# Causal mask of a two-layer decoder's self-attention: mask matmuls replaced by constant rows (first pass) and by a GpSimd select (second pass), constant rows copied on chip, the values' projection spread over the loop

## The reference

```python
# layer 0: 16 heads of 16, ALiBi bias; layer 1: 16 query heads, 4 key/value heads, no bias
x = x + attn0(layernorm(x))        # softmax(q k / 4 + slope*(j - i) + causal) v, then @ wo + bo
x = x + xattn0(layernorm(x), ctx)
x = x + moe0(layernorm(x))
x = x + attn1(layernorm(x))        # softmax(where(j > i, -inf, q k / 4)) v
x = x + xattn1(layernorm(x), ctx)
x = x + moe1(layernorm(x))
```

## Time and profile before

| | |
|---|---|
| runs | 1432.47, 1433.92, 1435.11 us; median 1433.92 |
| profiled execution | 1430.22 us, its span 1428.4 us, mean TensorE clock 0.906 |
| busy | PE 84%, PEld 59%, DVE 63%, ACT 47%, POOL 32% of the span |
| layer 0 self-attention | span 0 to about 240 us |
| layer 1 self-attention | span about 606 to 820 us |

### The profile page before, as it was taken

One profiled execution on the slowest core, in us unless ns is written; L12 is line 12 of the kernel. 1 busy time (PEld: TensorE's weight loads), 2 busy tenths in 40 slices (PEclk: granted clock), 3 DMA queues, 4 the chain that ended last, 5 costly groups with the idle time before them and its releaser, 6 DMA issues.

```text
span 1428.4 us, 25941 instructions
## 1 busy us (share of the span) xinstructions
PE 1205.4 (84%) x8255; PEld 839.2 (59%) x8255; DVE 897.5 (63%) x2622; ACT 673.9 (47%) x1412; POOL 461.7 (32%) x708
## 2 busy tenths in 40 slices
PE   3789998986699999848898768778787778999988
PEld 2467766765366666535565545555555554688855
DVE  3646654665333222266876578999999884566557
ACT  2245534321211111114454479999999991333310
POOL 1010101245611111111222234456555554255510
PEclk8899999997799999968999968987887888999999
DMA  6585751411211111144442030000000003354454
GB/s 139 115 208 120 148 150 39 148 38 60 87 45 45 45 52 46 48 139 123 116 140 71 3 122 2 2 32 32 24 21 20 32 32 122 95 158 158 158 177 144
DMA packets 71889, 123.43 MB, mean 86 GB/s; under 512 B 12630, under 2 KB 54998, under 8 KB 68255
## 3 DMA queue, kind: packets, MB, share of 16 engines
q1 hardware_dynamic: 59756, 91.76, 24.5%
q0 software_dynamic: 10272, 28.39, 5.5%
q10 hardware_dynamic: 1728, 1.61, 0.3%
HBM read 77.14 MB, written 44.19 MB: 85 GB/s over the span
## 4 chain that ended last, share of the span: by engine, by line
PE 53%; issue 12%; ACT 10%; DVE 9%; DMA 7%; POOL 6%; SPq 3%; POOLq 0%; DVEq 0%; ACTq 0%
PE ps L227 16%; PE ps L1092 15%; PE ps L1109 7%; ACT work L1806 5%; DMA W<-q_parts 3%; ACT work L1811 2%; POOL xs_scratch L1423 2%; DMA k_parts<-work 2%; PE ps L1101 2%; PE ps L1077 2%; DVE work L580 2%; POOL work L1837 2%; PE ps L444 2%; PE ps L1657 1%; SPq L791 1%
## 5 line engine op out<-in xcount | busy, mean ns | idle before, releaser
L1092 PE MATMUL ps<-W,work 128*128 x628 | 227.9, 496 | 1.4 <-issue 1.2
L1806 ACT ACTIVATE work<-ps,work 128x512 f32<-128x512 f32 x256 | 211.4, 873 | 8.8 <-POOL work L1837 7.2
L1441 POOL DMA_INDIRECT ys_scratch<-work x118 | 113.2, 960 | 260.7 <-DVE work L1285 112.4
L1742 DVE TENSOR_REDUCE work<-ps 128x1 f32<-128x512 f32 x256 | 172.9, 679 | 29.1 <-PE ps L1651 28.4
L580 DVE TENSOR_REDUCE work<-ps 128x2 f32<-128x512 f32 (+1 forms) x192 | 128.7, 684 | 91.3 <-PE ps L447 91.0
L1335 DVE TENSOR_TENSOR work<-work,ps 128x128 f32<-128x128 f32 (+1 forms) x118 | 49.7, 421 | 199.5 <-ACT work L1404 198.9
L688 ACT ACTIVATE work<-ps 128x512 f32<-128x512 f32 x192 | 114.6, 602 | 101.0 <-PE ps L467 98.6
L271 POOL TENSOR_TENSOR rstd<-ve,half 128x1 f32<-128x1 f32 x96 | 56.0, 587 | 294.8 <-DVE ve L267 292.3
L1092 PEld LDWEIGHTS ps<-W,work 128*128 128x128 f32 x628 | 111.0, 191 | 68.5 <-issue 62.0
L1811 ACT COPY work<-ps 128x1024 bf16<-128x1024 bf16 x128 | 141.0, 1101 | 7.7 <-PE ps L1657 7.6
L1837 POOL TENSOR_SCALAR work<-work 128x1 f32<-128x1 f32 x256 | 99.7, 390 | 134.3 <-DVE work L1742 119.8
(11 more groups left out here) (253 smaller groups left out, 2374.8 us busy)
## 6 DMA issues: line engine op xcount, KB each, us to landing
work<-xs_scratch SPq DMA_DIRECT2D x79, 132.0 KB, 2.1
W<-ys_scratch SPq DMA_DIRECT2D x16, 512.0 KB, 3.8
q_parts<-work SPq DMA_DIRECT2D x48, 128.0 KB, 1.7
W<-k_parts SPq DMA_DIRECT2D x48, 128.0 KB, 4.5
W<-q_parts SPq DMA_DIRECT2D x16, 384.0 KB, 6.2
W<-in_w_in SPq DMA_DIRECT2D x6, 1024.0 KB, 11.5
work<-xs_scratch SPq DMA_DIRECT2D x39, 130.0 KB, 2.1
W<-q_parts SPq DMA_DIRECT2D x16, 256.0 KB, 7.0
```

The source lines that it names most:

```text
L1092: mm = q.e.matmul(PS[bks[c]][:, 0:N], self.XT[s % 2][:, k, :], w[:, k, bass.ds(regs[s] + 512 * c if c else regs[s], N)], start=k == 0, sto ...
L1742: q.e.tensor_reduce(self.mm[:, h:h + 1], PS[banks.of["c1_s", t, h]][:, :], AX, ALU.max).then_inc(*up("c1_mx", t, h))
L1806: q.e.activation(self.ee[n // 2 % 3][:, 512 * (h % 2):512 * (h % 2) + 512], PS[banks.of["c1_s", t, h]][:, :], ACT.Exp, bias=self.nb[:, h:h ...
```

## The change

The mask matmuls of both passes go. In the first pass the mask is part of the contraction: rows 96 to 127 of the stack get constants that give 0 on the allowed pairs and a large negative number on the others, and the diagonal block is a matmul of its own, with 126 rows; the block left of it keeps 99 rows. In the second pass nothing is masked before exp; GpSimd sets the forbidden entries of the exponentials' diagonal blocks to 0 (`pool_keep`, 12 `affine_select` per element), and `pe_attend_v` waits for that. The bias takes 3 rows, not 6.

The 32 constant rows come once by two DMAs of 16 KB (`rowsQ`, `rowsK`) and are repeated over the heads on chip, three buffers each: ACT copies 32 x 4096 bf16 for q (`act_rows`, the first ahead of `ln_copy`), GpSimd 32 x 4096 (layer 0) or 32 x 1024 (layer 1) for k (`pool_rows`). Maximum rows overlap rows that the first pass needs at zero, so `sp_stack` has one more DMA from element 3 on (24 KB), and in layer 0 one for elements 0 to 2.

`pe_v` is cut in two and put at u = 0 and 1; `fin1` goes to u = 2, 3 (DVE 4, 5), `fin2` to 6, 7 (ACT 7, 8), `fin3` to 8, 9 (DVE 9, 10), GpSimd's part of them to u = 5, 6.

```diff
 def pe_scores(self, q, b, u):
-    q.wait_ge(at("stack", L, b, 5), at("rows", L, 2), at("consts", "all"), *free)
+    q.wait_ge(at("stack", L, b, 5), at("rowsq", L, b % 3), at("rowsk", L, b % 3), at("consts", "all"), *free)
     for i in range(n):
-        q.e.matmul(PS[bk][:, w * i:w * i + w], qs[0:NA, h, 128 * j:128 * j + 128], ks[0:NA, h // self.per, 0:w], ...)
-    q.e.matmul(ov[:, :, w - 128:w], idb[:, :], bc(maskQ[:, :], 1, n), ...)
+        if j == 1:
+            q.e.matmul(PS[bk][:, c0 - 128:c0], qs[0:NS, h, 128:256], k[0:NS, 0:128], ...)
+        mm = q.e.matmul(PS[bk][:, c0:c0 + 128], qs[0:NA, h, 128 * j:128 * j + 128], k[0:NA, 128 * j:128 * j + 128], ...)
 def pe_attend_s(self, q, b, g, kind):
-    q.e.matmul(ov[:, :, 0:128], idb[:, :], bc(maskK[:, :], 1, len(hs)), ...)
 def pe_attend_v(self, q, b, g):
-        q.wait_ge(at("exp", L, b, g, i // 2))
+        q.wait_ge(at("keep", L, b, g, i // 2))
+def act_rows(self, q, n):
+    q.wait_ge(at("one", 1), *self.base())
+    q.e.copy(self.qs[n][96:128, :, :], bc(rowsQ[96:128, :], 1, H)).then_inc(*up("rowsq", self.L, n))
 def scalar(self, q):
+    self.act_rows(q, 0)
     ln_copy(q, self.ln, 0)
...
             self.act_mid(q, i + 2, 1)
+        if i < 0:
+            self.act_rows(q, i + 3)
+def pool_keep(self, q, b, g, kind):
+    v = self.pt(b, g, kind).rearrange("p (i n) -> p i n", n=w)[:, :, 0:128]
+    q.wait_ge(at("exp", self.L, b, g, kind))
+    q.e.affine_select(out=v, in_=v, pattern=[[0, len(hs)], [1, 128]], compare_op=ALU.is_ge, fill=0.0, base=0,
+                      channel_multiplier=-1).then_inc(*up("keep", self.L, b, g, kind))
+def pool_rows(self, q, n):
+    q.wait_ge(at("one", 1), at("rowsk", self.L, n - 1), *self.base())
+    q.e.tensor_copy(self.ks[n][96:128, :, :], bc(rowsK[96:128, :], 1, self.NK)).then_inc(*up("rowsk", self.L, n))
 def gpsimd(self, q):
+    for n in range(3):
+        self.pool_rows(q, n)
+    q.wait_ge(at("rowsk", L, 2))
     for i in range(-2, B + 1):
-        if i >= 1: fin1 or fin2 of i - 1
         for u in range(12):
+            if 0 <= i < B:
+                self.pool_keep(q, i, u // 3, u % 3)
+            if i >= 1 and u in (5, 6): fin1 or fin2 of i - 1
 def sp_stack(self, q, b):
     q.wait_ge(at("wr", L, b, 1), at("stack", L, b - 1, 5), at("ps2", L, b - 3, 3, 2))
+    if L == 0 and b < 3:
+        q.e.dma_start(qs[96:99, :, :], I["c_rows"][0:3, :].bitcast(BF)).then_inc(*landing("stack", 0, b, -10))
+    if b >= 3:
+        q.e.dma_start(qs[101:104, :, :], I["c_rows"][3:6, :].bitcast(BF)).then_inc(*landing("stack", L, b, -10))
```

More of the change, by code:

```diff
@@ L177, in decoder @@
         work = sb("work", [128, 9700])
[L178 removed]
+        SM = sb("SM", [128, 5380])
         RS = 2048 + 128
@@ L426, in pe_qk, with pe_v @@
                 mm.then_inc(*up("qk", L, b, w))
-            def pe_v(self, q, b):
+            def pe_v(self, q, b, j):
                 L, wt, n = self.L, w_att[self.L], 16 * self.NK
                 c0 = 512 if L == 0 else 320
[L431 to L435, removed]
+                if j == 0:
+                    bk, free = banks.take(self.rp, ("vv", L, b), [("V", L, b)])
+                    q.wait_ge(*free)
+                mm = pair_mms(q, PS[banks.of["vv", L, b]][:, n * j:n * j + n], [(xnt(2 * b + j)[k], wt[:, k, c0:c0 + n]) for k in range(2)])
+                if j == 1:
+                    mm.then_inc(*up("vv", L, b))
@@ L442, in pe_scores @@
                 for i in range(n):
                     h = h0 + i
[L444 to L448, removed]
+                    k, c0 = ks[:, h // self.per, :], w * (i + 1) - 128
@@ L1999, in constants, with words @@
     slopes = np.array([start * start ** h for h in range(H)], np.float32) * np.float32(4)
-    pos = np.arange(S, dtype=np.float32)
-    rows = np.ones((15, H, S), np.float32)
-    rows[3:6] = pos
+    pos = np.arange(S)
+    rows = np.zeros((6, H, S), np.float32)
     for c in range(3):
-        rows[6 + c] = part(slopes[:, None] * pos[None, :])[c]
-        rows[9 + c] = -part(slopes)[c][:, None]
-    bits = (rows.reshape(15, H * S // 2, 2).view(np.uint32) >> 16).astype(np.uint32)
-    return {"c_sq": sq, "c_rows": (bits[:, :, 0] | (bits[:, :, 1] << 16)).view(np.float32)}
+        rows[c] = part(slopes)[c][:, None]
+    one = np.zeros((2, 32, S), np.float32)
+    one[1, 0:3] = pos
+    for t in range(2):
+        one[0, 3 + t] = np.where((pos >= 128 * t) & (pos < 128 * t + 64), -2.0 ** 99, 0.0)
+        one[1, 3 + t] = np.where((pos >= 128 * t + 64) & (pos < 128 * t + 128), 1.0, 0.0)
+    one[1, 5:8] = 1.0
+    own, at = pos % 128 // 6, pos % 128 % 6
+    for n in range(22):
+        one[0, 8 + n] = np.where(own < n, -2.0 ** 80, np.where(own == n, -2.0 ** (59.0 - 21.0 * at), 0.0))
+        one[1, 8 + n] = np.where(own == n, 2.0 ** (21.0 * at - 63.0), 0.0)
+    def words(v):
+        bits = (np.ascontiguousarray(v).reshape(v.shape[0], -1, 2).view(np.uint32) >> 16).astype(np.uint32)
+        return (bits[:, :, 0] | (bits[:, :, 1] << 16)).view(np.float32)
+    return {"c_sq": sq, "c_rows": words(rows), "c_one": words(one.reshape(64, S))}
 _OUT = ((2048, 256), "float32")
```

108 lines of the change are left out of this document (51 added, 57 removed).

## The result

The changed kernel takes 1445.65 us (median of 4 runs, 1443.74 to 1447.78), beside 1434.41 us for the kernel before on the same chip (4 runs): ratio 1.0081, 95% interval 1.0063 to 1.0099. That is slower by 11 to 12 us, where 1428 us, a gain of some 6 us, was forecast. The time lies inside the given range of 1410 to 1451 us, but the change went the other way. The profiled execution took 1447.78 us, its span is 1445.9 us.

The account below looks back on a forecast made before the run. The stack's read-back loop was to cap layer 0 and DVE to pace layer 1. Layer 0's -0.5 and layer 1's -5.7 us took 1430.2 to 1424.0; 3.7 us from profiled execution to median gave 1428, range 1410 to 1451.

Parts of the forecast that it names:

- rival 1: GpSimd's slow select decides, from about 1.0 us per 256 columns, via layer 1 and second-pass tails: 1454 us, 17%.
- mask matmuls gone: Less TensorE work in both layers: -8.0 us in layer 0's turns, -8.7 us from DVE's idle time in layer 1.
- select: Layer 1: GpSimd's selects, 8.8 us per element, mostly hide; holding up DVE costs +3 us.
- start: Opening of layer 0: ACT's and GpSimd's row copies and one more DMA delay it, +4.5 us (0.5 to 9).
- order of the work: Moving `pe_v` and `fin1` into the u steps, where PE waits for DVE: no cost of its own counted.
- TensorE's clock: Layer 0: longer gaps bring one more start at half clock, +3 us (0 to 14).
- the cap: Layer 0: the stack's read-back loop, 23.5 to 24.0 us a turn, limits the gain whatever PE's load.
- Rival 3: TensorE was the bound, so layer 0 follows PE and layer 1's DVE is not held up: 1413 us, 13%.
- slack of 2.7 and 1.0 us: Layer 0, elements 3 and 4: the margin between TensorE's pace and the stack's loop.
- spreads the gaps: Moving `pe_v` and `fin1` spreads TensorE's gaps, so only one more half-clock start is counted, +3 us.
- DVE held up by selects: Layer 1: selects delay DVE in `dve_lo` and the layernorm's scalar operations, 0.5 us in six iterations, +3 us.
- rival 2: The clock gives the gain back: layer 0's turns all start at half speed, short gaps slow layer 1: 1438 us, 20%.

Follow-up runs that it names:

- e3_start: Changed kernel with ACT's first row copy behind the layernorm's copy and GpSimd's copies held until after element 1's `dve_lo`: 1436.73 us, ratio 1.0019.
- e12_warm: e6_order_start plus five unread 512-column matmuls where TensorE waits for the stack in layer 0: 1431.13 us, ratio 0.9984.
- e8_before_merged: Kernel before, with the six reads of k parts issued as three that repeat their source: 1510.97 us, ratio 1.0526.
- e9_e6_merged: e6_order_start with the six reads of k parts issued as three that repeat their source: 1517.49 us, ratio 1.0557.
- e10_mask2_matmul: e6_order_start with the second pass masked by its old matmul instead of the select: 1422.99 us, ratio 0.9926 to the kernel before.
- e7_no_select: e6_order_start without GpSimd's selects, second pass unmasked: 1423.40 us, ratio 0.9914 to the kernel before.
- e1_order_back: Changed kernel with the old order of the work on all four engines: 1436.91 us, ratio 1.0034 to the kernel before.
- e14_values_spread: e10_mask2_matmul with only the values' projection spread in two halves: 1424.00 us, ratio 0.9928 to the kernel before.
- e15_finish_late: e10_mask2_matmul with only `fin1` and what follows it moved late: 1434.16 us, ratio 1.0005 to the kernel before.
- e11_dead_selects: e6_order_start with all selects issued on memory nothing reads, second pass's diagonal blocks unmasked: 1431.68 us, ratio 0.9968.
- e17_act_copy_first: e10_mask2_matmul with ACT's first row copy ahead of the layernorm's copy again: 1429.17 us, ratio 0.9969 to the kernel before.
- e5_no_mask: Kernel before without its two mask matmuls, scores unmasked, nothing else changed: 1420.21 us, ratio 0.9898.
- e16_e10_again: e10_mask2_matmul repeated unchanged as a base: 1423.72 us, ratio 0.9925 to the kernel before.
- e6_order_start: Changed kernel with the old order of the work and the start's row copies moved later: 1432.94 us, ratio 0.9984 to the kernel before.

## Why the prediction was wrong

That 1445.65 us lies inside the range is luck. The range's slow end was set by rival 1's mechanism, which is not what happened, and the forecast's own range ended at 1435.

The ratios form a chain in which each kernel differs from the one ahead by one step: no masks 0.9898, plus the row machinery 0.9914, plus selects 0.9984, plus the early copies 1.0034, plus the new order 1.0081. In us of 1434, beside the forecast's terms:

| step | forecast | measured |
|---|---|---|
| mask matmuls gone | -8.0 and -8.7 = -16.7, rows' DMA in it | -14.6, and +2.3 for rows and DMA (not resolved from 0) |
| select | +3 | +10.0 |
| start | +4.5 (0.5 to 9) | +7.2, by `e3_start` 9 |
| order of the work | 0 | +6.7 |
| TensorE's clock | +3 | in the rows above; in layer 0 under what `e12_warm` resolves |
| sum | -6.2 | +11.6 |

**Right: the cap.** Of 56 us, 17 were to reach the time and 12 to 15 did. Turns in layer 0 were to be about 23.3 us and are 23.3 and 23.4, with PE waiting for the stack at their ends; `e8_before_merged` and `e9_e6_merged` show the loop from its other side. Rival 3, TensorE as the bound, is out: no kernel here came near 1413 us. Once the first pass's mask is gone, taking off the second's adds nothing that these intervals resolve: `e10_mask2_matmul`, with half the mask matmuls back, has the gain of `e7_no_select`. A small slip lies in the slack of 2.7 and 1.0 us. The 9.10 us of landing count from the start of the last read's issue, not from its end, so the slack is about 0.4 us more for each. The forecast's waits at elements 3 and 4 did not come.

**Wrong: "spreads the gaps", at no cost.** This is the step that failed outright: the term for the order of the work was 0, and it measured 6.7 us. The text took moving `pe_v` and `fin1` to be about gaps on TensorE, and named no cover that goes. A PSUM bank that `fin1` fills is emptied by DVE's part of the same step, which moved to u = 4; the next taker of the ring in layer 1 is the kv matmul. The queues' code shows this (the ring of three banks, and its takers), the trace of before does not, since the wait is new. The forecast looked for waits on engines and transfers and left out buffers. That wait is shown, 4.33 us; that it is the whole of the 6.7 us is not. In layer 0 there is the cover that goes. The three transfers of the maximum's rows are issued at 85.77 us in the changed kernel and at 85.42 in `e1_order_back`, and the second pass starts at 93.84 and 93.51, but TensorE waits 3.14 us for it in the first and 0.76 in the second, where `pe_v` and `fin1` stand ahead of it. With either of the two moved alone (`e14_values_spread`, `e15_finish_late`) that wait is absent, but it is absent in their base as well, so what it costs by itself is open.

**Wrong by size: the select.** The price was too high and the effect too low: +3 was forecast and 10 us measured. 128 x 0.44 and 64 x 0.64 us are 97 us, against 141 by the 8.8 us per element I took, and 0.44 us is below the 1.0 us from which rival 1 was to decide. Rival 1 had the right side, slower, but by another road, and its 1454 us was too much: its place was the value product behind a slow select, and `e11_dead_selects` shows most of the cost with no value product behind it. The term I did write, "DVE held up by selects ... 0.5 us in six iterations", fits the trace as a mechanism, though not in `dve_lo`: the layernorm's operation and the residual's are longer beside the selects, and the wait for GpSimd's powers grew. The 0.5 us was a guess; it should have been counted by operation and by wait.

The Trainium skill, "SBUF — State Buffer", section "Who interferes with whom", names as contending a GpSimd instruction that reads SBUF and a DVE instruction with two SBUF inputs. The first trace that shows it agrees: `dve_lo` 4.78 instead of 1.46 us beside GpSimd's copies. The 1.90 us that the forecast held beside it are of another kind, a DVE operation with one tensor as input beside memsets, which read nothing.

**Wrong by size: the start.** The forecast was 4.5 us and the runs have 7.2 to 9. ACT's copy was to put the projection at 13.7 us, 2.6 late; it starts at 12.26, but against the same kernel without the early copy that is not 1.1 but about 3 us late (3.1 in `e17_act_copy_first`). Of GpSimd's copies, 1.5 us was taken for `dve_lo`, and the pair lost 3.3. The bounds, 0.5 to 9, held. I missed two things. ACT's second copy, for element 1, sits before another transpose (20.58 us above). And the change in the loads, with six row DMAs fewer, seems to give something: the first projection waited for the bias to 11.13 us, in `e5_no_mask` with the same loads to 12.79, and with the new loads and ACT out of the way it starts at 9.76 (`e16_e10_again`) and 8.82 (`e6_order_start`). No run changes the loads alone. If so, ACT's early copy takes a gain as well as time.

**The clock.** Four of the first score groups in layer 0 took 1.03 us for eight matmuls, where the one at 161.04 took 0.62 us, so rival 2 had its rows. Its price was not found in layer 0, with the old order; in layer 1 it was not looked for.

## What to carry to other kernels

When an engine's step is moved, list what it holds (PSUM banks, rings, buffers) until its last part on another engine, and who takes them next: a step that only looks spread can delay the release. Work moved to an idle GpSimd can still be paid for, in DVE operations that run beside it and in small powers or chains queued behind it; 97 us of selects cost 10 us here. And split a change before judging it: here the rows in the first pass were worth 0.7%, while the select, the early copies and the late finish each took 0.5 to 0.8%.

## What the runs showed of the hardware

- GpSimd's affine select of a 128-row float32 tile takes 0.44 us for 256 columns and 0.64 for 512 (on bf16, in `e11_dead_selects`, 0.43 and 0.64), at the low ends I had used (0.40 and 0.65), not between them and the high ones.
- Reads whose source has the number of copies (3, 2, 1) as its outermost dimension were much worse here than six plain reads: the same stack lands 18.86 us after the last issue instead of 9.10, with the DMA engines busy to 0.17 to 0.20 in the last 8 us, and the kernel is 5.3% slower.
- Mask matmuls of 256 and 512 columns in the second pass, 28 us of them, cost nothing measurable where the stack (layer 0) or DVE (layer 1) sets the pace (0.9926 with, 0.9914 without, intervals overlapping); the granted clock of layer 1 was 0.84 with and 0.80 without.
